# A Fourier-domain MLP on 128x128 images: the half-height matmuls of two column groups in one stretch, image unfolding in half-size steps

## The reference

```
xf = rfft2(x, axes=(1, 2), norm='ortho').reshape(B, H, W // 2 + 1, 8, 96)
xr, xi = xf.real, xf.imag
o1r = relu(xr @ w1[0] - xi @ w1[1] + b1[0])      # per block, 96x96
o1i = relu(xi @ w1[0] + xr @ w1[1] + b1[1])
o2r = o1r @ w2[0] - o1i @ w2[1] + b2[0]
o2i = o1i @ w2[0] + o1r @ w2[1] + b2[1]
o   = softshrink(stack([o2r, o2i]), 0.01)
out = irfft2(complex(o), s=(128, 128), norm='ortho') + x
```

## Time and profile before

| | |
|---|---|
| median of 3 runs (lowest, highest) | 5099.5 us (5099.32, 5104.72) |
| span of the profiled execution, first to last instruction | 5094.2 us |
| PE busy | 4981.3 us (98%) |
| DVE busy | 3816.7 us (75%) |
| ACT busy | 2996.3 us (59%) |
| POOL busy | 1436.3 us (28%) |
| mean granted TensorE clock | 0.993 |
| HBM traffic | 83 GB/s over the span |

### The profile page before, as it was taken

One profiled execution on the slowest core, in us unless ns is written; L12 is line 12 of the kernel. 1 busy time (PEld: TensorE's weight loads), 2 busy tenths in 40 slices (PEclk: granted clock), 3 DMA queues, 4 the chain that ended last, 5 costly groups with the idle time before them and its releaser, 6 DMA issues.

```text
span 5094.2 us, 113221 instructions
## 1 busy us (share of the span) xinstructions
PE 4981.3 (98%) x40000; PEld 4673.3 (92%) x40000; DVE 3816.7 (75%) x6159; ACT 2996.3 (59%) x5409; POOL 1436.3 (28%) x905
## 2 busy tenths in 40 slices
PE   6999999999999999999999999999999999999997
PEld 6999999999999999999999999999999999999996
DVE  5777777777777777777777777777777777777876
ACT  4555655556655566555566555665556655556653
POOL 3033223332123332233321333312333123332220
PEclk8999999999999999999999999999999999999998
DMA  5044423444323443234442344432344323444233
GB/s 114 12 94 105 98 59 69 91 105 105 68 57 87 105 105 87 56 81 94 105 105 52 70 90 105 106 70 62 79 105 106 86 61 78 92 105 105 61 73 72
DMA packets 1699712, 430.24 MB, mean 84 GB/s; under 512 B 1698848, under 2 KB 1698976, under 8 KB 1699104
## 3 DMA queue, kind: packets, MB, share of 16 engines
q1 hardware_dynamic: 1696768, 421.83, 37.5%
q10 hardware_dynamic: 2336, 0.59, 0.1%
HBM read 220.84 MB, written 201.33 MB: 83 GB/s over the span
## 4 chain that ended last, share of the span: by engine, by line
PE 96%; DVE 2%; issue 1%; SPq 1%; ACT 0%; DMA 0%; DVEq 0%; ACTq 0%
PE psum L807 15%; PE psum L778 14%; PE psum L822 14%; PE psum L760 13%; PE psum L849 13%; PE psum L832 9%; PE psum L790 7%; PE psum L859 3%; PE psum L860 3%; PE psum L861 3%; DVE mixed L655 1%; SPq L387 1%; DVE spectrum L628 0%; PE psum L840 0%; PE psum L839 0%
## 5 line engine op out<-in xcount | busy, mean ns | idle before, releaser
L655 DVE COPY mixed<-psum 128x768 f32<-128x768 f32 (+1 forms) x512 | 477.4, 932 | 700.0 <-PE psum L790 700.0
L541 ACT ACTIVATE sums_high<-psum 128x512 fp32r<-128x512 f32 x768 | 459.2, 599 | 731.3 <-PE psum L849 731.2
L807 PEld LDWEIGHTS psum<-mats,mixed 128*128 128x128 f32 x6272 | 744.0, 191 | 121.2 <-issue 113.1
L807 PE MATMUL psum<-mats,mixed 128*128 128x128 f32 x6272 | 841.8, 283 | 0.0
L778 PE MATMUL psum<-w_whole,whole 128*128 128x192 f32 x4160 | 782.3, 330 | 40.9 <-ACT whole L482 11.4
L822 PE MATMUL psum<-w2t,hidden 128*128 128x192 f32 x4160 | 771.7, 328 | 0.0
L849 PE MATMUL psum<-mats,spectrum 128*128 128x128 f32 x6144 | 743.7, 275 | 3.1 <-DVE spectrum L663 1.6
L760 PE MATMUL psum<-mats,x 128*128 128x128 f32 x6144 | 704.9, 277 | 33.6 <-DVE x L582 17.8
L760 PEld LDWEIGHTS psum<-mats,x 128*128 128x128 f32 x6144 | 696.0, 193 | 40.9 <-issue 23.0
L778 PEld LDWEIGHTS psum<-w_whole,whole 128*128 128x128 f32 x4160 | 673.3, 197 | 60.6 <-issue 33.7
L849 PEld LDWEIGHTS psum<-mats,spectrum 128*128 128x128 f32 x6144 | 714.5, 192 | 4.1 <-DVE sums_low L701 2.0
(11 more groups left out here) (76 smaller groups left out, 7800.7 us busy)
## 6 DMA issues: line engine op xcount, KB each, us to landing
x<-x SPq DMA_DIRECT2D x736, 192.0 KB, 2.9
out<-x SPq DMA_DIRECT2D x736, 192.0 KB, 2.5
x<-x SPq DMA_DIRECT2D x736, 64.0 KB, 2.6
out<-x SPq DMA_DIRECT2D x736, 64.0 KB, 2.2
x<-x SPq DMA_DIRECT2D x32, 144.0 KB, 2.7
out<-x SPq DMA_DIRECT2D x32, 144.0 KB, 2.3
w2t<-L_conv_w SPq DMA_DIRECT2D x124, 36.0 KB, 1.8
x<-x SPq DMA_DIRECT2D x64, 48.0 KB, 2.4
```

The source lines that it names most:

```text
L655: copied = dve.tensor_copy(mixed[s % 2][:, 0:k], both_b(s)[:, 0:k])
L807: last = pe.matmul(out[tile], flat[:, tile * SIZE:(tile + 1) * SIZE], mat(FH), start=True, stop=True)
```

## The change

PE's steps become rounds (`ROUNDS` = 10) of an even and the odd group around it. In a round j the order is: C of group 2j-2, whole part of B of 2j-1, outer part of D of 2j-3, whole part of B of 2j, C of 2j-1, outer part of D of 2j-2, and then one stretch of 64-row matmuls: B of 2j, D of 2j-2, D of 2j-1, B of 2j+1. Even groups still begin B with the whole part and end with the halved one; odd groups begin with the halved part and end with the whole one, and D likewise the other way round. `start` and `stop` of the accumulation, the semaphores `b_done` and `d_done` and the waits on `b_copied` and `seeded` move with that. DVE and ACT get their lists in rounds too, and `gather` is split into `gather_whole` and `gather_halved`. `unfold_step` is cut once more, into 16 half steps of 640 or 768 elements; four stand in each of the rounds 1 to 4 (`spare`), and the weight steps follow in rounds 5 and 6. The arithmetic is the same.

```diff
@@ PE: stage_b_whole, stage_b_halved (stage_d_outer and stage_d_middle likewise)
             def stage_b_whole(par, n, s):
+                opens = s % 2 == 0
...
-                elif s >= 2:
+                elif opens:
 
                     pe.wait_ge(b_copied, n * NS + (s if s > 2 else 1))
                 pe.wait_ge(whole_gathered, n * NS + (s + 1))
...
             def stage_b_halved(par, n, s):
+                opens = s % 2 == 1
                 if s == 0:
                     pe.wait_ge(first_halved, n + 1)
                 else:
+                    if opens and s > 1:
+                        pe.wait_ge(b_copied, n * NS + s)
                     pe.wait_ge(halved_gathered, n * (NS - 1) + s)
...
@@ PE: layers
-                for s in range(NS + 2):
-                    if s < NS:
-                        stage_b_whole(par, n, s)
-                    if s == NS:
+                for j in range(ROUNDS):
+                    if j == 1:
+                        stage_b_whole(par, n, 1)
+                    if j == ROUNDS - 1:
+                        stage_d_outer(par, n, odd_group(j - 2))
+                    if even_group(j - 1) is not None:
+                        stage_c(n, even_group(j - 1))
+                    if j > 1 and odd_group(j - 1) is not None:
+                        stage_b_whole(par, n, odd_group(j - 1))
+                    if j < ROUNDS - 1 and odd_group(j - 2) is not None:
+                        stage_d_outer(par, n, odd_group(j - 2))
+                    if even_group(j) is not None:
+                        stage_b_whole(par, n, even_group(j))
+                    if odd_group(j - 1) is not None:
+                        stage_c(n, odd_group(j - 1))
...
+                    if even_group(j - 1) is not None:
+                        stage_d_outer(par, n, even_group(j - 1))
+
+                    if even_group(j) is not None:
+                        stage_b_halved(par, n, even_group(j))
+                    if even_group(j - 1) is not None:
+                        stage_d_middle(par, n, even_group(j - 1))
+                    if odd_group(j - 1) is not None:
+                        stage_d_middle(par, n, odd_group(j - 1))
+                    if odd_group(j) is not None:
+                        stage_b_halved(par, n, odd_group(j))
@@ DVE: unfold_step, and layers
-                x_unit, (lo, hi) = xs[par], PIECES[k // 2]
+                p, what = divmod(k, 4)
+                x_unit, (lo, hi) = xs[par], PIECES[p]
+                lo, hi = ((lo, lo + 5), (lo + 6, hi))[what % 2]
...
+                for j in range(ROUNDS):
+                    if even_group(j - 1) is not None:
+                        hide_middle(even_group(j - 1))
+                    if 0 < j:
+                        spare(4 * j - 4)
+                    if odd_group(j - 1) is not None:
+                        mix(odd_group(j - 1))
+                    if 0 < j:
+                        spare(4 * j - 3)
+                    if odd_group(j - 2) is not None:
+                        shrink(odd_group(j - 2))
+                    if odd_group(j - 1) is not None:
+                        seed(odd_group(j - 1))
+                        hide_middle(odd_group(j - 1))
+                    if 0 < j:
+                        spare(4 * j - 2)
+                    if even_group(j) is not None:
+                        mix(even_group(j))
+                    if even_group(j - 1) is not None:
+                        shrink(even_group(j - 1))
+                    if even_group(j) is not None:
+                        seed(even_group(j))
+                    if 0 < j:
+                        spare(4 * j - 1)
```

More of the change, by code:

```diff
@@ L469, in _, with gather_whole @@
         def _(act):
-            def gather(s):
-                w, h, first = whole[s % 2], halved[s % 2], GROUPS[s][0]
+            def gather_whole(s):
+                w, first = whole[s % 2], GROUPS[s][0]
+                j = 2 + 2 * first
                 if s == REAL:
@@ L509, in layers @@
                 act.wait_ge(dve_copied, (n + 1) * len(A_DVE))
-                gather(0)
+                gather_whole(0)
                 act.wait_ge(w_loaded[par], (m + 1) * W_LOADS * 16)
-                for s in range(NS + 2):
[L513 to L534, removed]
@@ L535, in layers, with hide @@
-                act.wait_ge(flip_done, n + 1)
-                act.activation(U[:, 0:BLOCK, SIZE + 2:].rearrange("p c k -> p k c"), bank_flip,
-                               ACT.Copy).then_inc(flip_copied, 1)
+                def hide(t):
+                    tiles = hidden[t % 2]
+                    act.wait_ge(c_done, n * NS + (t + 1))
+                    act.activation(tiles[:, 0, 0:pairs(t)], bank_c[:, 0, 0:pairs(t)], ACT.Relu,
+                                   bias=b1t[par][:, 0:1]).then_inc(relu_done, 1)
+                    k = pairs(t) if None not in GROUPS[t] else 1
+                    act.activation(tiles[:, 1, 0:k], bank_c[:, 1, 0:k], ACT.Relu,
+                                   bias=b1t[par][:, 2:3]).then_inc(relu_done, 1)
@@ new lines, in hide_middle, with shrink @@
+                def hide_middle(t):
+                    dve.wait_ge(c_done, n * NS + (t + 1))
+                    dve.tensor_scalar(middle[t % 2][:, 0:pairs(t)], middle_c[:, 0:pairs(t)], b1t[par][:, 1:2], 0.0,
+                                      ALU.add, ALU.max).then_inc(middle_done, 1)
+                def shrink(t):
+                    rows, j = rows_d(t), 2 + 2 * GROUPS[t][0]
+                    dst = real_kw[:, :, :] if t == REAL else U[:, 0:BLOCK, j:j + rows]
+                    dve.wait_ge(excess_done, n * NS + (t + 1))
+                    dve.scalar_tensor_tensor(dst, parts_d(t), LAMBDA, excess[:, :, 0:rows], op0=ALU.add,
+                                             op1=ALU.min).then_inc(shrunk, 1)
@@ L733, in _ @@
                 add(1, UNITS - 1, q)
-            for k in range(2 * NP):
+            for k in range(4 * NP):
                 unfold_step(UNITS - 1, 1, k)
@@ L777, in stage_b_whole @@
                 for k in columns(s):
-                    pe.matmul(bank_b(s, k), whole[s % 2][:, k // 2, :, k % 2], w1_whole[par][:, :, :].rearrange("p r o -> p (r o)"),
-                              start=k % 2 == 0, stop=False, skip_group_check=True)
+                    last = pe.matmul(bank_b(s, k), whole[s % 2][:, k // 2, :, k % 2], w1_whole[par][:, :, :].rearrange("p r o -> p (r o)"),
+                                     start=opens and k % 2 == 0, stop=not opens, skip_group_check=True)
+                if not opens:
+                    last.then_inc(b_done, 1)
             def stage_b_halved(par, n, s):
+                opens = s % 2 == 1
                 if s == 0:
@@ L816, in stage_d_outer @@
             def stage_d_outer(par, n, s):
+                ends = s % 2 == 1
                 pe.wait_ge(relu_done, n * (2 * NS) + (2 * s + 1))
[L818 removed]
+                if not ends:
+                    pe.wait_ge(seeded, n * NS + (s + 1))
                 for k in columns(s):
```

166 lines of the change are left out of this document (97 added, 69 removed).

## The result

| | before | after |
|---|---|---|
| median (lowest, highest) | 5099.41 us (5098.2, 5104.72) | 5182.07 us (5178.6, 5194.21), 4 runs |
| ratio, 95% interval | 1 | 1.0162 [1.0147, 1.0176] |
| span of the profiled execution | 5094.2 us | 5176.8 us |
| mean granted clock | 0.993 | 0.991 |

A forecast was written before the change was run, and what follows sets the result against it. PE, busy 98% of the span, was taken as the bound. Per unit 4.2 us saved and 5.65 added, 44 us in all, plus 22 for clock falls, on 5099.5 gave 5165 us, range 5098 to 5200.

The forecast's parts named there:

- the visits: PE's switches into and out of 64-row matmuls: 0.39 us each, nine fewer a unit, saving 3.5 us a unit.
- The copies of B: A group's first B matmul waits for the copy of the last sums: 1.39 us to cover, 0.09 lost at nine places.
- The start of a unit: C of group 1 on PE waits 2.2 us for DVE's relu, half step and copies; 1.2 in the first unit.
- Rounds 2 and 4: PE waits for DVE's copy behind half steps: 1.07 us in round 2, 0.78 in round 4.
- Round 6: Weight steps stand in both places on DVE; PE's wait taken as 0.4 us, between nothing and 0.78.
- Round 5: Holds one short weight step on DVE; PE's wait put at 0.09 us.
- The clock: Idle of some 1.9 us at a unit's start halves PE's clock for 3.41 us: 13 falls in 31 units, +22 us.
- 1: The clock holds: the idle size that brings a fall may lie above 1.9 us; 5143 us, chance 0.22.
- 2: The clock falls in every unit, as all idles have the same place and nearly the same length; 5196 us, chance 0.08.
- 3: Half steps fit into DVE's idle time, costing less than the line says; faster, 5060 us, chance 0.11.
- 4: Waits a little smaller: half step 0.87 us, no wait at the nine places of 0.09; 5104 us, chance 0.08.
- 5: The 0.39 us belongs to each block of 64-row matmuls, not the visit, so nothing is saved; 5277 us, chance 0.03.

## Why the prediction was right, and where it was not

**What bounds the kernel, and the visits: right.** Nine visits fewer at 0.39 were to save 3.5 us a unit. The loads that stand idle at a change of form fell from 33 a unit to 17 (544 and 516 before, 316 and 224 after, by 32 units), about to half, as from the 38 to the 20 of the forecast. The chip gave 0.405 for a visit when 15 were added, and with DVE's list in order the unit shrank by 2.13, which is the 4.2 of saved visits and old waits less what stays: 0.55 at the unit's start, 0.42 in round 2 and twelve bare weight loads of 0.09 to 0.10.

**The copies of B: right.** The loop of 1.39 us showed as forecast: L844 behind a D block takes 1.40 to the next block for 1.31, so 0.09 is lost, in rounds 3 and 7 (in 8, with six records, 1.06 for 0.98); L861 loses 0.10 in rounds 3 to 7. The halved part of round 2 loses 0.42 for 0.4 (at 1048.44 in the kernel after: 0.16 of idle time, 0.16 of the tail of the record ahead and 0.10 of a bare load).

**The start of a unit: right.** L844 to L879 is 2.83 us in the mean of the 31 units that unfold, 2.18 more than its work, and 0.08 is lost behind it: 2.26 for 2.2. The half step is 949 ns for the 970 of the line; groups by shape of the kernel after:

```profile
L635 DVE TENSOR_TENSOR x<-x 128x768 f32<-128x768 f32 x224 | 212.4, 949 | 0.1
L640 DVE SCALAR_TENSOR_TENSOR x<-x 128x768 f32<-128x768 f32 x224 | 212.3, 949 | 0.0
...
L654 DVE TENSOR_SCALAR w2t<-w2t 64x96 f32<-64x96 f32 x64 | 47.6, 744 | 1.0
L654 DVE TENSOR_SCALAR w2t<-w2t 32x96 f32<-32x96 f32 x64 | 41.2, 644 | 2.0
```

**Rounds 2 and 4: right.** 1.07 for 1.07 (0.97 from L896 to L844, 0.10 behind it) and 0.75 for 0.78.

**Round 6: mis-sized.** "Between nothing and 0.78 I take 0.4." It is 0.99 in units without a half-clock stretch, and up to 2.0 between L896 and L844; with 30 units that is +18 us, most of the 25 by which the waits came out too low. The step that failed is the price of the two weight steps: the forecast weighed them as something between none and a half step and had no term for what holds them, though the trace before had their groups by shape with means far above the 0.2 us that one takes alone:

```profile
L615 DVE TENSOR_SCALAR w2t<-w2t 32x96 f32<-32x96 f32 x64 | 52.1, 814 | 2.0
L615 DVE TENSOR_SCALAR w2t<-w2t 64x96 f32<-64x96 f32 x64 | 36.4, 568 | 1.0
```

The timeline of all engines in the kernel after shows what happens:

```profile
1085.17 1.54 POOL L451 TENSOR_TENSOR x<-x 128x640 f32<-128x640 f32 x1
...
1085.69 1.08 DVE L654 TENSOR_SCALAR w2t<-w2t 32x96 f32<-32x96 f32 x1
...
1086.80 0.96 DVE L693 COPY mixed<-psum 128x768 f32<-128x768 f32 x1
1087.00 1.54 POOL L456 TENSOR_TENSOR x<-x,doubled 128x640 f32<-128x640 f32 x1
1087.79 0.81 DVE L654 TENSOR_SCALAR w2t<-w2t 64x96 f32<-64x96 f32 x1
```

The step at 1085.69, 96 numbers wide, ends at 1086.77, just behind POOL's operation (1086.71), and the copy stands behind it. The kernel without the fold shows that POOL's folding is what holds it.

**Round 5: mis-sized, a little.** Put at 0.09, it is 0.25, +5 us. The forecast counted one short weight step; ahead of that copy stands the last half step of round 4 too, and with the half steps away the loss is 0.08.

**The clock: right in kind, a little too many.** Forecast were 13 stretches of 1.7 us, +22. The profiled execution has nine more than before inside the `layers` sections, eleven stretches in ten units for two, and a unit with one is 1.94 longer (0.15 of it in round 6): about 16 us. One of them in the kernel after, timeline of PE and the stretches around it (columns as the earlier trace rows):

```profile
390.91 0.82 PE L844 MATMUL psum<-w_whole,whole 128*128 128x192 f32 x4
393.74 2.40 PE L879 MATMUL psum<-mats,mixed 128*128 128x128 f32 x12 [2.00 <-DVE mixed L691]
395.94 2.33 PE L896 MATMUL psum<-w2t,hidden 128*128 128x192 f32 x8
```

```profile
390.90:394.30 3.40, 1.40 (x11) 1.14 (x10) 3.18 (x7) 2.91 (x6) 0.00 (x0) 1.00 0.00 0
394.30:397.70 3.40, 3.40 (x16) 3.40 (x15) 2.25 (x4) 0.84 (x2) 0.00 (x0) 0.50 0.01 2
397.70:401.00 3.30, 3.30 (x34) 2.86 (x33) 1.12 (x2) 1.49 (x3) 0.00 (x0) 1.00 0.00 0
```

After 2.00 us of idle the clock is at 1.2 GHz for 3.4 us, and L879 takes 2.20 to the next block instead of 1.41. How many units have one changes from run to run of like kernels (10 here, 21 with the other weight form), and the four runs of the kernel after had granted clocks of 0.991, 0.990, 0.990 and 0.988, of which the profiled one was the fastest. So this term could be given no better than as a range.

**The sum.** Forecast 44 us of waits and 22 of clock. Measured in the `layers` sections: 84.9, of which about 16 clock; of the other 69, 44 were in the forecast, 18 are round 6, 5 round 5, and 2 stay spread over small places. The stages outside, forecast at +0.8, came out at -2.3. So the waits were forecast 25 too low; the clock, 6 too high, and the stages outside, 3 too high, hid a third of that, and the 17 us of the total look better than the terms are.

**The rivals.** 1 and 2: neither, ten units of thirty-one. 3: no, the half step kept to the line; the kernel with the half steps away (5068) shows what it would have given, near the 5060 put. 4: no, the half step was 0.95 and the small waits were there. 5: no, by the visits' measured price.

## What to carry to other kernels

A saving on the bound engine is worth only what the engines that feed it can follow: write down, for each thing that it waits for, what stands ahead of it in the other engine's list, and put that one first among what is ready. Here the same PE order was 1.6% slower or 1.5% faster than before, by DVE's list alone. And small operations with a mean far above their size in the groups by shape are waiting for something: find out for what before giving them a price.

## What the hardware showed that I had not expected

**DVE's weight steps, which read and write SBUF alone, wait for POOL.** In the kernel after, 35 of the L654 steps ran with POOL idle, 205 ns each; 93 ran beside an operation of POOL, 878 ns in the mean and up to 1583, and 90 of these ended within 0.1 us of POOL's operation. Copies, softshrinks and relus with an operand in PSUM took the same time with and without POOL (a copy L693 of 768 elements 955 and 958 ns). The Trainium skill (SBUF — State Buffer, section "Terms") says that DVE and GpSimd contend for a pair of SBUF ports which one holds for a whole instruction while the other stands still; the trace agrees in the waiting, 0.2 us that became 1.08 under a POOL operation of 1.54, and does not show the ports. The change to two inputs did not get around it (688 and 724 ns). The half steps never ran beside POOL, so for these it isn't shown.

**The clock falls behind some idles of a size and not behind others.** Thirty-one start waits of 2.0 us brought it down in 10 units of one kernel and in 21 of another; behind the start waits of 1.2 us of the kernel with the half steps away it fell in none. What decides it was not found; filling the wait with matmuls ended it.
